# A four-layer graph network in one kernel: its batch loop written out, and the order of its passes changed around the row norms, the last queries and keys, and the exponentials

## The reference, cut to what matters

```
x = ln(x + L0(x)); x = ln(x + L1(x)); x = ln(x + L2(x)); x = ln(x + L3(x))     # ln: layernorm, last axis
L0: q, k, v = x Wq.T, x Wk.T, x Wv.T
    rel = adj.T * (q k.T);  rel = rel / norm(rel, last axis);  rel v
L1: norm_adj = adj * deg^-1/2 (rows and columns);  norm_adj (x W) + bias
L2: h = x; three times:
      a = adj h (the same matrix in and out)
      z = sigmoid(w3 a + u3 h + b);  r = sigmoid(w4 a + u3 h + b)
      hv = tanh(w5 a + u5 (r * h) + b);  h = (1 - z) h + z hv
L3: 8 heads of 32: softmax(q k.T / sqrt(32) + (1 - adj) * -1e9) v, then Wo and bias
```

## Time and profile before

| | |
|---|---|
| median of 3 runs | 2481.36 us (2473.95 to 2492.97) |
| the profiled execution | 2486.78 us |
| its span, first to last instruction | 2485.0 us |
| mean granted TensorE clock | 0.936 |
| busy | PE 87%, PE weight loads 69%, DVE 62%, ACT 51%, POOL 41% |
| passes by the first `W_g` matmul of each | begin at 27.3, 148.4, 286.4, 433.8, ... 2217.6 us |

### The profile page before, as it was taken

One profiled execution on the slowest core, in us unless ns is written; L12 is line 12 of the kernel. 1 busy time (PEld: TensorE's weight loads), 2 busy tenths in 40 slices (PEclk: granted clock), 3 DMA queues, 4 the chain that ended last, 5 costly groups with the idle time before them and its releaser, 6 DMA issues.

```text
span 2485.0 us, 37970 instructions
## 1 busy us (share of the span) xinstructions
PE 2164.2 (87%) x12214; PEld 1708.5 (69%) x12214; DVE 1528.4 (62%) x3423; ACT 1267.3 (51%) x2500; POOL 1009.4 (41%) x1154
## 2 busy tenths in 40 slices
PE   5889989898889989888898889989888898889965
PEld 4667676776767767676777767767676776767743
DVE  5556576665657656575665756656575665756632
ACT  3335555464554636555464554636455464555644
POOL 3024444344343434444344443534444344443533
PEclk8999999899999999999999999999999999999977
DMA  3011020111202121030111202021020111202030
GB/s 114 1 48 37 18 69 25 37 43 36 60 19 47 31 53 43 19 69 27 35 43 37 58 19 58 20 52 43 19 68 27 35 43 40 55 19 60 18 78 16
DMA packets 65657, 101.77 MB, mean 41 GB/s; under 512 B 11424, under 2 KB 31136, under 8 KB 65440
## 3 DMA queue, kind: packets, MB, share of 16 engines
q1 hardware_dynamic: 65440, 98.87, 15.7%
HBM read 23.34 MB, written 8.39 MB: 13 GB/s over the span
## 4 chain that ended last, share of the span: by engine, by line
issue 42%; PE 29%; POOL 19%; DVE 5%; ACT 3%; POOLq 1%; DMA 0%; SPq 0%; DVEq 0%; ACTq 0%
POOL fa L308 8%; PE ps L850 7%; POOL rsum L302 6%; PE ps L851 6%; PE ps L852 6%; PE ps L872 4%; PE ps L952 2%; POOL fa L354 2%; PE ps L966 1%; POOL rstd L297 1%; ACT fa L401 1%; ACT pT L396 1%; POOL ra L272 1%; DVE stats L627 1%; DVE xn L772 1%
## 5 line engine op out<-in xcount | busy, mean ns | idle before, releaser
L302 POOL TENSOR_TENSOR rsum<-esum,mhalf 128x2 f32<-128x2 f32 x256 | 195.3, 763 | 971.0 <-ACT fa L401 971.0
L672 DVE CUSTOM_DVE_ANT_0 fa<-ps,mask 128x512 f32<-128x512 f32 x512 | 332.2, 686 | 263.0 <-PE ps L938 260.5
L952 PE MATMUL ps<-ident,fa 128*128 128x128 f32 x2048 | 342.7, 293 | 170.1 <-POOL fa L308 102.0
L308 POOL TENSOR_SCALAR fa<-fa,rsum 128x512 f32<-128x512 f32 x512 | 442.8, 877 | 52.7 <-POOL rsum L302 52.7
L952 PEld LDWEIGHTS ps<-ident,fa 128*128 128x128 f32 x2048 | 253.0, 149 | 286.9 <-issue 91.5
L396 ACT COPY pT<-ps 128x512 f32<-128x512 f32 x512 | 298.9, 584 | 267.0 <-PE ps L952 265.8
L401 ACT ACTIVATE fa<-fa,nmax 128x512 f32<-128x512 f32 x512 | 366.3, 723 | 38.8 <-DVE nmax L672 38.8
L659 DVE TENSOR_TENSOR ra<-ps,ra 128x512 fp32r<-128x512 f32 x224 | 152.4, 689 | 347.2 <-ACT ra L494 181.5
L872 PE MATMUL ps<-adjT,ra 128*128 128x512 f32 x1024 | 269.8, 419 | 20.5 <-DVE ra L782 13.1
L872 PEld LDWEIGHTS ps<-adjT,ra 128*128 128x128 f32 x1024 | 204.4, 202 | 74.3 <-DVE ra L782 18.5
L938 PE MATMUL ps<-ra 128*128 128x512 f32 x512 | 188.8, 451 | 2.2 <-ACT vf L467 1.2
(11 more groups left out here) (183 smaller groups left out, 4738.9 us busy)
## 6 DMA issues: line engine op xcount, KB each, us to landing
ra<-ra SPq DMA_DIRECT2D x512, 128.0 KB, 2.4
fa<-in_x_T SPq DMA_DIRECT2D x17, 512.0 KB, 5.7
fa<-in_x SPq DMA_DIRECT2D x17, 512.0 KB, 5.2
out<-fa SPq DMA_DIRECT2D x16, 512.0 KB, 4.1
fa<-in_L_gnn_w_w SPq DMA_DIRECT2D x3, 512.0 KB, 8.2
adj_n<-in_adj SPq DMA_DIRECT2D x1, 1024.0 KB, 5.5
fa<-in_L_gnn_u_w SPq DMA_DIRECT2D x2, 256.0 KB, 9.2
fa<-in_L_gnn_Wk SPq DMA_DIRECT2D x1, 256.0 KB, 5.7
```

The source lines that it names most:

```text
L302: nc.gpsimd.tensor_tensor(rsum[:, 2 * k:2 * k + 2], esum[:, 2 * k:2 * k + 2], mhalf[:, 4:6], ALU.pow).then_inc(rs_r, 1)
L308: nc.gpsimd.tensor_scalar(SC[:, g], SC[:, g], rsum[:, 2 * k + u:2 * k + u + 1], 1.0, ALU.mult, ALU.mult).then_inc(nrm, 1)
L672: nc.vector.tensor_tensor_reduce(out=SC[:, s % RING], in0=ps[:, 4 + u], in1=mask[:, 2 * (k % 8 // 4) + u], scale=-1.0, scalar=3.0e38, op0= ...
L952: ins = nc.tensor.transpose(dst[:, a, u * P:(u + 1) * P], SC[:, (2 * k + u) % RING, kt * P:(kt + 1) * P], ident[:, :])
```

## The change

- `passes` is a Python loop: all 18 passes are straight code on every engine, and waits are on constants.
- The squares are made half by half (two instructions of 128x1024), POOL makes one addition for each half, and PE adds the two halves in PSUM (16 small matmuls where there were 8). They stand between `qk_of(0)` and `qk_of(1)` instead of in the middle of the products with `W_wv0`.
- The statistics of the first two norms are taken half by half: each half is added, measured and given to POOL before the next one.
- `qk_of(2)` and `qk_of(3)` go from ahead of the values' product to behind `score(1)`, after layer 1's products. `back(t, 0, ...)` stands behind them. Slots 2 and 3 of `STK` are filled after them.
- In step 0 of layer 2 the chunks come one place later: `score(2)` stands behind the gather, `score(3)` in the middle of `w4`, and so on, up to `score(7)` behind `values`. The exponentials on ACT follow.
- The cast of `AB0` and that of h (`HTS`) stand ahead of `exponentials(1)` and `(2)`.
- `exponentials(15)` and with it the row sums of that chunk go from the start of the next pass to the end of step 2.

```diff
-        QK_BANK = (6, 7, 6, 7)
+        QK_BANK = (6, 7, 0, 1)
...
-        def passes(eng, body):
-            body(0, None, None)
-            body(1, 0, None)
-            with eng.Fori(0, B - 2) as it:
-                body(it + 2, it + 1, it)
-            body(None, B - 1, B - 2)
-            body(None, None, B - 1)
+        def passes(body):
+            for k in range(B + 2):
+                body(*[b if 0 <= b < B else None for b in (k, k - 1, k - 2)])
...
                         if n == 2:
-                            sp.wait_ge(vv_ps, t + 1)
+                            sp.wait_ge(qk_ps, t * 4 + 4)
...
             def squares(i):
-                gp.wait_ge(sq_f, i + 1)
-                for s in range(1, NT):
-                    nc.gpsimd.tensor_tensor(REL[:, 0], REL[:, 0], REL[:, s], ALU.add).then_inc(sq_s, 1)
-                    if s < NT - 1:
-                        gp.wait_ge(sq_s, i * (NT - 1) + s)
+                for c in range(2):
+                    gp.wait_ge(sq_f, i * 2 + (c + 1))
+                    nc.gpsimd.tensor_tensor(REL[:, 2 * c], REL[:, 2 * c], REL[:, 2 * c + 1], ALU.add).then_inc(sq_s, 1)
...
-                    act.wait_ge(rel_l, i * 2 + 2)
-                    nc.scalar.activation(REL[:, :, :], REL[:, :, :], ACT.Square).then_inc(sq_f, 1)
+                    for c in range(2):
+                        act.wait_ge(rel_l, i * 2 + (c + 1))
+                        nc.scalar.activation(REL[:, half(c)], REL[:, half(c)], ACT.Square).then_inc(sq_f, 1)
...
-                def statistics(which, x, k, sums):
...
+                def sums_and_statistics(k, ready, scale, x):
                     for c in range(2):
-                        after(which, sums[c])
...
+                        dve.wait_ge(ready, i * 2 + (c + 1))
+                        for s in (2 * c, 2 * c + 1):
+                            ins = STT(xg[:, s], natural(2)[:, s], scale[:, s:s + 1], x[:, s], ALU.mult, ALU.add)
+                        after("g", mark("g", ins))
+                        variance("g", k, c, aggregate("g", k, c, stats_of("g", xg, k, c)))
...
                     qk_of(0)
-                    qk_of(1)
+                if i is not None:
+                    pe.wait_ge(u_l, i * 2 + 1)
+                    pe.wait_ge(sq_s, i * 2 + 2)
+                    for s in range(NT):
+                        for c in (0, 2):
+                            ins = mm(ps[:, 0, s:s + 1], REL[:, c, s * P:(s + 1) * P], ones1[:, :],
+                                     start=c == 0, stop=c == 2)
+                    ins.then_inc(ssq_ps, 1)
+                if t is not None:
+                    qk_of(1)
...
                         if j > 0:
                             u3_of(j)
+                        elif t is not None:
+                            pe.wait_ge(qk_l, t * 4 + 4)
                         gather(XNS, xn_l, m + 1, a_ps)
```

More of the change, by code:

```diff
@@ L361, in body @@
                     xT_lo(i + 1)
-            passes(gp, body)
+            passes(body)
         @block.scalar
@@ L488, in body @@
                     m = None if i is None else i * 6 + 2 * j
+                    if t is not None and j == 1:
+                        exponentials(t, Z)
                     if t is not None and j > 0:
@@ L546, in body @@
                         prob_copy(t, B_, 1)
-            passes(act, body)
+            passes(body)
         @block.vector
@@ L733, in body @@
                         dve.wait_ge(s_pool, wd_l + ND)
[L734 to L744, removed]
+                    sums_and_statistics(0, o_ps, rnorm, XIN)
                 if i is not None:
@@ L767, in body @@
                     dve.wait_ge(xb_r, i + 1)
[L768 to L774, removed]
+                    sums_and_statistics(1, o1_ps, dinv, xg)
                 if t is not None:
-                    masked(1)
+                    qk_lo(2)
+                    qk_lo(3)
                 if i is not None:
@@ L839, in body @@
                                    ALU.subtract).then_inc(xn_l, 1)
+                    if t is not None and j == 0:
+                        masked(E)
                 for which, (s, b, per) in chains.items():
                     assert b is None or count[which] == per, (which, count[which])
-            passes(dve, body)
+            passes(body)
         @block.tensor
@@ L931, in score @@
                         pe.wait_ge(stk[slot], t * 128 + 64 * (k // 8 + 1))
-                    if k == 0:
-                        pe.wait_ge(vv_r, t + 1)
+                    if k == 0 and o is not None:
+                        pe.wait_ge(x4a, o + 1)
                     for u in range(2):
@@ L1083, in body @@
                     score(1)
+                    qk_of(2)
+                    qk_of(3)
                     back(t, 0, 0)
                     back(t, 0, 1)
-                    score(2)
                 if i is not None:
@@ L1120, in body @@
                     if t is not None and j == 0:
-                        back(t, 1, 1)
-                    if i is not None:
-                        for d in range(DT):
+                        back(t, 1, 0)
+                    for d in range(DT):
+                        if i is not None:
                             pe.wait_ge(a_l, m + (d + 1))
@@ L1128, in body @@
                                     ins.then_inc(r_ps, 1)
+                        if t is not None and j == 0 and d == 0:
+                            back(t, 1, 1)
+                            score(3)
                     if t is not None:
                         back(t, Z, 0)
-                        score(A if j == 0 else B_)
+                        if j > 0:
+                            score(B_)
                     if i is not None:
@@ L1138, in body @@
                         back(t, Z, 1)
-                        score(B_ if j == 0 else C)
-                    if i is not None:
-                        for q in range(DT):
+                        score(A if j == 0 else C)
+                    for q in range(DT):
+                        if i is not None:
                             pe.wait_ge(r_t, m + (q + 1))
@@ L1145, in body @@
                             ins.then_inc(z_ps, 1)
-                    if t is not None:
+                        if t is not None and j == 0 and q == 0:
+                            back(t, D_, 0)
+                            score(B_)
+                    if t is not None and j > 0:
                         back(t, D_, 0)
-                        if j == 0:
-                            score(C)
                     for d in range(DT):
@@ L1163, in body @@
                         back(t, A, 1)
+                        if j == 0:
+                            score(E)
                     if i is not None:
```

83 lines of the change are left out of this document (36 added, 47 removed).

## The result

The changed kernel takes 2325.65 us (median of 4 runs, 2324.82 to 2327.76) and the kernel before 2479.98 us beside it (2473.95 to 2492.97): a ratio of 0.937, 95% interval 0.933 to 0.941. I had 2368 us, in a range from 2320 to 2425. The direction and the range held; the gain was a third larger than the forecast, and what came true is close to rival (2), the clock that stays up, to which I had given 0.15.

What follows compares the result with a forecast made beforehand. The prediction took the kernel to be bound by TensorE and what it waits for; its terms 62 + 52 - 5 + 7 = 116 us off 2486.8 gave 2370.8, taken as 2368 us for the median, range 2320 to 2425.

Steps and rivals of the forecast that it cites:

- rival (2): Whole pass: the clock stays up and chains overlap better, 1.7 + 1.5 us a pass more, 2320 us; chance 0.15.
- Straight passes: Loop turns on all engines: 45.9 us of idle time and 16 us of slow first matmuls go, sum 62 us.
- rival (4): Anywhere in a pass: straight code fetched late, 3.5 us each time; 2480 us with two a pass, 2592 with four; chance 0.04.
- Exponentials of chunk 15: Pass start: the 2.90 us wait for POOL and the lower clock behind it go, 3.7 x 14 passes = 52 us.
- the last three and the 0.3: Small terms summed per pass: -0.95 + 2.3 - 1.4 - 0.3, about -0.3 us, 15 passes, -5 us.
- Squares and row norms: Small matmuls on PE, 16 for 8: norm no sooner where it matters, nothing gained and 0.95 us a pass lost.
- half-by-half norms: Chain from first sums to split: 8.4 us becomes 7.6, between 0.8 gained and 1 lost; 1.2 us new waiting at first gather.
- rival (3): Ahead of the first gather: the row norm does come sooner and 1.2 us goes, 15 x 1.2, 2350 us; chance 0.1.
- Queries and keys behind layer 1: Hole of 2.84 us behind layer 1 filled: 4.4 us idle becomes 1.2 + 2.5, net gain 2.3 us a pass.
- step 0 one chunk later: Step 0 of layer 2: PE waits about 1.7 us ahead of `back(3, 1)`, not 0.35; cost 1.4 us, 0 to 5.
- The ends: Outside the passes: 4.5 us saved at each of two starts, 2 in pass 0, less 4 in the end stretch: +7 us.
- The signs: Changed profile: no "issue", mean clock 0.97 or so, passes 140 to 141 us, POOL's scaling wait near 30, 1.5 to 2 ahead of `back(3, 1)`.

Runs made afterwards that it cites:

- experiment 1: The kernel before with its batch loop written out as straight passes, nothing else changed: 2418.18 us, ratio 0.974.
- experiment 4: The changed kernel with the hardware loop put back on all engines: 2451.47 us, ratio 0.988.
- experiment 11: The kernel of experiment 4 with 160 idle instructions ahead of the loop on TensorE: 2400.82 us, ratio 0.967.
- experiment 3: The kernel of experiment 2 with the squares and the norms' statistics made half by half: 2365.34 us, ratio 0.953.
- experiment 7: The changed kernel with DVE's copy of the sums of squares ahead of the low part of key 1: 2315.00 us, ratio 0.931.
- experiment 2: The kernel of experiment 1 with chunk 15's exponentials moved to the end of step 2: 2360.46 us, ratio 0.951.
- experiment 5: The changed kernel with chunk 15's exponentials put back to the start of the next pass: 2384.24 us, ratio 0.958.
- experiment 6: The changed kernel with chunk 2's scores back ahead of the eight transposes and chunk 1's masking ahead of the norm's last step: 2360.98 us, ratio 0.949.

## Why the prediction was right, and where it was off

- *Straight passes:* 62 us booked, 64 measured in experiment 1, with 48 of idle time for 45.9. Shown. The row had the price. The 51 and 108 ns for a branch of the Trainium skill (Advanced Engine Details and Errata, Control Flow Timing) did not have it. The price belongs to that loop in that place, though: experiments 4 and 11 show 126 and some 52 us for others. I had taken 3.5 us as the cost of a turn in general, in rival (4) too. Pass 2, which I called straight, is the loop's first; it has no turn ahead of it, and the argument from it stands.
- *Exponentials of chunk 15:* 52 booked, 58 and 59 measured in two orders. Shown. Idle time was less than I had (27 us in thirteen passes, where 34 were booked, since TensorE now waits 0.5 us for the other batch's normed rows), the clock more (21 us for 14). The 0.3 us for the late copies was taken off twice in the sum, in the 3.7 and again among "the last three and the 0.3", which makes the forecast 4.5 us too slow.
- *Squares and row norms:* "nothing is gained and 0.95 lost" was right in kind. Experiment 3 has +5 us for it and the half-by-half norms together, where the two terms of my working gave between 2 us and 29 us. That the order on DVE is what holds the norm back is shown by experiment 7, which brings 11 of the 18 us that rival (3) had hoped for from the change as it is.
- *Queries and keys behind layer 1, and step 0 one chunk later:* this is the step that was off. Booked +2.3 and -1.4 us a pass, 13.5 us; measured 40. In the thirteen passes it is 36.8 us for 11.7 booked, and both parts fell short. Idle time makes 17.6 of the missing 25 us: 9.1 more was booked (0.7 saved and 1.4 lost a pass), 8.5 less was measured. The single waits came close (ahead of the first gather 1.08 for 1.2; behind layer 1 0.82 + 0.87 + 0.17 = 1.9 for 2.5; ahead of `back(3, 1)` 1.25 for 1.7), but all on the good side, and one thing was missing: "the end of the step hangs on the chain of h as before". The waits for h fell from 38.3 us in experiment 3 to 31.5 (L1158 there, L1167 in the changed kernel), nearly all of it in step 0, so step 0 cost about 0.4 us a pass and not 1.4. The clock makes the other 7.5: 20.8 us booked in thirteen passes, 28.3 measured. "I leave 1.7 of it, since the pieces lie close together" was too much: the clock stayed up behind the pieces in eleven of the thirteen passes, where the hole of 2.84 us had lowered it, and the gather went from 5.76 to 3.97 us.

```profile
PE ps L1158 <- DVE fa L814: 38.3, 67, 3.4
```

- *The ends:* the stretch behind pass 14's end fell by 13.3 us (267.4 to 254.1), for 9 us booked at the starts of the passes without a batch `i`, 3.7 in pass 15, and 4 lost.
- *The clock in all:* I booked 55 us, and the Trainium skill's rule of below 1% (TensorE: Matmul & The Clock Gate, Part 1), which is said there of the ramp in a typical kernel, would have had 25. The measured fall of busy time in thirteen passes is 62 us, with small matmuls added: the rule does not hold for this kernel, which had three holes of 2.5 to 4.3 us in each pass.
- *Rival (2)* came closest in time (2320), and the clock did stay up. But the clock is only half of what was missing: in the thirteen passes idle time fell by 86 us and busy time by 62, where my terms come to 67 and 38.
- *The signs:* no "issue", a mean clock of 0.977 and about 1 us ahead of the first gather came as written. Passes are 137.1 us and not 140 to 141, the wait for POOL's scaling 12.0 and not near 30, the one ahead of `back(3, 1)` 1.25 and not 1.5 to 2. One sign of being wrong came true and says nothing: ACT and DVE end TensorE's waits in step 0, but they did so in the kernel before as well.

## What to carry to other kernels

Before costing a filled gap, look at what the clock does behind it: here one wait of 2 to 5 us in each pass cost TensorE a third to four fifths of the added idle time again in slower matmuls (experiments 1, 2, 4, 5 and 6), and waiting in pieces under 1 us mostly cost only itself, though experiment 7 shows that it doesn't always. A hardware loop on the engine that bounds a kernel has a price at each turn that changes with the code around it (some 52 to 126 us in one kernel, about 6 us on the four other engines together), so write it out there, or measure it at more than one offset. When work is moved to fill a hole, follow its products to their reader: without the later scores the hole would have moved to SP's DMAs.

## What was not expected of the hardware

- The turn of a loop on TensorE was one wait of 3.5 us in one order, 4.8 and 1.4 us in another, and after 160 more instructions ahead of the loop none in four turns of thirteen and 4.7 us in the others. Behind the four, a whole pass ran without one block of TensorE's code being fetched.
- Less waiting can come with more low clock: experiment 7 removed 16 us of idle time and added 8 us of busy time in thirteen passes. The cause stays open.
